# Router stage of a fused attention and expert kernel: rows split in place, 16-bit turning, residual kept unscaled

## The chip, the cores and the metric

One Trainium2 chip, one core of it. The metric is the device time of one execution in microseconds (us). Engines are named as in the profile: PE (TensorE, with PEld for its weight loads), DVE (VectorE), ACT (ScalarE), POOL (GpSimd) and SP (SyncE, which here only issues DMAs).

## What is computed

The kernel computes a whole two-layer model over 2048 tokens of 512 numbers. What matters here is the last block, the mixture of experts, and how it is fed:

```python
# x: the residual after layer 1's attention, [2048, 512]
x = _layernorm(x_in)                     # handed to the block
aff = sigmoid(x @ wa)                    # wa: [512, 16]
topk_p, topk_i = top_k(aff, 2); topk_p /= sum(topk_p)
routed = sum over the two chosen experts of topk_p * expert(x)
shared = sum over two shared experts of expert(x)
expert(x) = w2(gelu(x @ g + gb) * (x @ w1 + b1)) + b2
return x_in + (x + shared + routed)      # so the residual and the normed row are both added
```

With m the mean and r the inverse deviation of a row, the normed row is `r*x_in - m*r`, so what is added to the experts' results is `(1 + r)*x_in - m*r`. The kernel calls `1 + r` the gain and `-m*r` the shift.

## The kernel before, in words

The kernel is a row of stages, each a block in which every engine runs its own program and engines meet by semaphores; between two stages all engines meet. The tokens are 16 tiles of 128. In order: long convolution, a ternary feed-forward, keys and values, attention (`stage_attention`, L1575), the router (`stage_router`, L2044), a stage that chooses experts and runs the two shared ones (`stage_route_and_shared`, L2199), and the routed experts in 47 blocks of 128 rows (`stage_experts`, L2624). The residual x lies in SBUF (`x_res`, 16 tiles of 128x512 f32) until the router ends; then its space becomes that of the experts' weights.

Products of wide numbers are made of two 16-bit parts, a high one and a low one (value minus high), with three matmuls (`three_products`, L1138): high by high, high by low, low by high.

**Attention.** The order of work is a list of steps (batch, unit) that all engines walk. Per batch SP loads the keys (L1654) and stacks the next queries in twelve small DMAs (`qs`, L1662), which PE needs for the first scores of the next batch (L1859). DVE adds the projection to x (`added`, L1781) and takes statistics (`statistics`, L1785). In the last batch it makes the means, scales and the first two normed tiles (`front`, L1547 to L1572).

**Router.** For tile t of 16:
- DVE makes `xn` (128x512 f32, two buffers) from x, mean and inverse deviation (L1571), two tiles ahead.
- ACT copies it to 16 bits, `rows` high (L2182); DVE takes the rest, `rows` low (L2125). SP stores both to `token_rows` in HBM (256 KB a tile, L2091), from which the expert stage later gathers. There are four buffers of rows (`SETS = 4`); ACT waits for the store of tile t-4.
- PE turns `xn` with four f32 transposes (L2158) into PSUM `ps_rx`. ACT copies that once as f32 (`r_xT`, L2186) and once as 16-bit high (`s_xT`, L2189); DVE takes the low (L2127). SP stores both parts of the first 12 tiles (`turned_tiles`, L2094).
- PE multiplies `r_xT` with the router's weights `wa` in f32, 16 columns, four matmuls (L2164, "xcount" in the profile is eight a tile).
- ACT makes gain*x + shift (L2193): in place for ten tiles, which SP stores to `mid_rows` (L2097); six tiles (chunks 6, 7 and 0) go to places that outlive x: `e_rows`, `s_x`, `e_yo`.

Beside it SP loads `wa` (L2078), the rows of biases (L2081, L2083) and six shared weights of 512 KB (L2086), which POOL casts to the high part (L2110) and DVE takes the low part of (L2131). At the end ACT makes exp of the logits (L2195) and DVE the sigmoid (L2145, L2146) and the low part of the biases (L2149).

**Later.** The shared experts' sum is added to x tile by tile on DVE (`add_sums`, L2427; for the two late chunks `add_shared`, L2847), the routed results in `add_results` (L2854, L2856). The biases of the down products come in by a product of a row of shares per token (`cols`, turned by PE) with `down_bias`.

```python
        self.xn = [sb(f"r_xn{i}", [P, D], F32) for i in range(2)]
...
                act.activation(scaled_x, k.x[:, t, :], ACT.Identity, bias=shift[:, t:t + 1], scale=gain[:, t:t + 1]).then_inc(added, 1)
```

Of the kernel before, what the change touches and what calls it, by code (L numbers as in the profile page):

```python
# [15 lines left out]
P = 128  # L16
# [1524 lines left out]

FRONT = 4
# [4 lines left out]
class RouterScales:  # L1547


    def __init__(self, sb, semaphore):  # L1550
        self.mean, self.var, self.tmp, self.rstd, self.gain, self.shift = (
            sb(f"r_{n}", [P, NT], F32) for n in ("mean", "var", "tmp", "rstd", "gain", "shift"))
        self.xn = [sb(f"r_xn{i}", [P, D], F32) for i in range(2)]
        self.var_ready, self.rstd_ready, self.scaled, self.xn_ready = (
            semaphore(f"rs_{n}") for n in ("var", "rstd", "sca", "xn"))

# [13 lines left out]
    def normalise(self, dve, x, t):  # L1570
        dve.tensor_scalar(self.xn[t % 2][:, :], x[:, t, :], self.mean[:, t:t + 1], self.rstd[:, t:t + 1], ALU.subtract, ALU.mult)\  # L1571
           .then_inc(self.xn_ready, 1)  # L1572


def stage_attention(k, ks, last_keys, v_hi, v_lo, qw, ow, vectors, x_mean, x_rstd, stats, qs, kb, ahead, front):  # L1575
# [3 lines left out]
    with ExitStack() as ctx:  # L1579
# [127 lines left out]
        def _(act):  # L1707
# [14 lines left out]
            for b, u in STEPS:  # L1722
# [23 lines left out]
                if u == 1 and queried(b + 2):  # L1746
                    act.wait_ge(shift_ready, 1)
                    for t in range(TPB):
                        tile = (b + 2) * TPB + t
                        act.activation(xn[t][:, :], xtile(tile), ACT.Identity, bias=x_shift[:, tile:tile + 1],  # L1750
# [257 lines left out]
E_N = 16  # L2008
SH_N = 2
FE = 256  # L2010
# [10 lines left out]
SETS = 4  # L2021
# [19 lines left out]
TURNED_STORES = EARLY[0] * ST  # L2041


def stage_router(k, stats, xaff, sgu, sd, down_bias, kept, front, x_places):  # L2044
# [4 lines left out]
    with ExitStack() as ctx:  # L2049
        sb = lambda name, shape, dt: ctx.enter_context(nc.sbuf_tensor(name, shape, dt))  # L2050
        two = lambda name, shape, dt: [sb(f"{name}{i}", shape, dt) for i in range(2)]
        wa = sb("r_wa", [P, DC, E_N], F32)
        gain, shift, xn, scaled, xn_ready = front.gain, front.shift, front.xn, front.scaled, front.xn_ready
        xT = two("r_xT", [P, DC, P], F32)
        rows = [sb(f"r_rows{i}", [P, 2, D], BF16) for i in range(SETS)]
# [3 lines left out]
        psX = [ctx.enter_context(nc.psum_tensor(f"ps_rx{i}", [P, D], F32)) for i in range(SETS)]  # L2059
        psL = ctx.enter_context(nc.psum_tensor("ps_rl", [P, NT * E_N], F32))  # L2060
        raw = [sb(f"r_raw{i}", [P, 1024], F32) for i in range(6)]
        w_loaded, w_high = [k.semaphore(f"r_w{i}") for i in range(6)], k.semaphore("r_whi")
        rows_high, rows_low = k.semaphore("r_rh"), k.semaphore("r_rl")
# [3 lines left out]
        wa_loaded, dve_step, added, x_psum, xT_ready, x_high, x_low, logits, exped = (  # L2067
            sem(n) for n in ("wa", "dve", "add", "xp", "xT", "xh", "xl", "log", "ex"))
        bias_zeroed, bias_loaded, bias_high, x_stored = (sem(n) for n in ("bz", "bl", "bh", "xst"))
        rows_stored, turned_stored = ([sem(f"{n}{i}") for i in range(SETS)] for n in ("rs", "ts"))  # L2070
        block = ctx.enter_context(nc.Block())
        chunks = lambda a: a.rearrange("p (c t) -> p c t", c=DC)
# [4 lines left out]
        def _(sp):  # L2077
            sp.dma_start(wa[:, :, :], k.ins["L1_ffn_wa"].rearrange("(c p) e -> p c e", p=P)).then_inc(wa_loaded, 16)  # L2078
            sp.wait_ge(bias_zeroed, 1)
# [4 lines left out]
            for n in range(6):  # L2084
# [29 lines left out]
        def _(dve):  # L2114
# [37 lines left out]
        def _(pe):  # L2152
# [937 lines left out]
```

## Time and profile before

| | |
|---|---|
| median of 3 runs | 1137.9 us (1137.3 to 1138.25) |
| profiled execution | 1144.85 us, its span 1143.1 us |
| PE / PEld busy in the span | 1029.8 us (90%) / 771.7 us (68%) |
| DVE / ACT / POOL busy | 845.9 us (74%) / 684.2 us (60%) / 582.2 us (51%) |
| mean granted clock of TensorE | 0.944 of full |
| DMA | 194.60 MB, mean 170 GB/s |

Times in rows are from the start of the span. "Busy" is the time in which an engine has an instruction in hand; a row's duration includes the fill and the drain, so instructions that follow each other closely overlap a little, and the distance between two starts is what one costs its engine. "Granted clock" is the share of TensorE's full 2.4 GHz that it was given. A bracket behind a row is the idle time before it and who ended that.

### The profile page before, as it was taken

Reading aid. Unit: us, or ns where it says so; the run is one execution under the profiler, and the core shown is the slowest. Engines: PE = TensorE matmul, PEld = TensorE weight load, DVE = VectorE, ACT = ScalarE, POOL = GpSimd, SP = SyncE. Lnnn points to the kernel's source line nnn. Section 1 sums busy time; section 2 is a strip of 40 time slices with the busy share of each in tenths; the row PEclk is TensorE's granted clock in tenths of the full one; section 3 lists DMA queues with packets and bytes.
Section 4 is the critical chain, followed back from the end, with each engine's and each line's share of the span. In section 5 each row is a group of like instructions: output and inputs, shape, how many; then the busy total and the mean of one; then the engine's idle time right before and its main releaser. Section 6 shows DMA issues by size and latency. Waiting matters only on the chain. (4 is left out here: it accounts for less than half of the span.)

```text
span 1143.1 us, 24593 instructions
## 1 busy us (share of the span) xinstructions
PE 1029.8 (90%) x9092; PEld 771.7 (68%) x9175; DVE 845.9 (74%) x1480; ACT 684.2 (60%) x1203; POOL 582.2 (51%) x635
## 2 busy tenths in 40 slices
PE   4899998689998998878999988789996999999997
PEld 4677776634443776557877766687673888888874
DVE  5589999869998788757888866698746455556548
ACT  4565773779886656567888764574543345545431
POOL 5444445425544344458778885303873355555520
PEclk9999999789999999979999998659999899999999
DMA  8584431869886223232222210764986577678879
GB/s 318 176 256 122 160 116 38 158 174 237 221 226 177 87 72 104 68 89 56 65 71 63 57 30 1 257 226 181 203 249 224 165 239 242 236 246 281 303 264 352
DMA packets 133705, 194.60 MB, mean 170 GB/s; under 512 B 67990, under 2 KB 70204, under 8 KB 132792
## 3 DMA queue, kind: packets, MB, share of 16 engines
q1 hardware_dynamic: 117256, 149.45, 43.3%
q0 software_dynamic: 8544, 24.68, 7.0%
q10 hardware_dynamic: 7792, 18.96, 5.3%
q8 instruction: 71, 1.16, 0.4%
q14 instruction: 42, 0.34, 0.1%
HBM read 127.47 MB, written 44.48 MB: 150 GB/s over the span
## 5 line engine op out<-in xcount | busy, mean ns | idle before, releaser
L470 PE MATMUL ps_y<-kv,toep 128*128 128x288 f32 x640 | 156.5, 407 | 5.2 <-DMA toep<-taps_padded 3.2
L470 PEld LDWEIGHTS ps_y<-kv,toep 128*128 128x128 f32 x640 | 121.2, 190 | 40.0 <-DMA toep<-taps_padded 4.7
L164 POOL TENSOR_TENSOR kv<-kx 128x1024 f32<-128x1024 f32 x32 | 60.6, 1893 | 85.9 <-DVE outT L524 37.7
L1808 DVE TENSOR_REDUCE at_negmax<-ps_s 128x4 f32<-128x1024 f32 x64 | 78.1, 1220 | 32.0 <-PE ps_s L1859 32.0
L2684 POOL DMA_INDIRECT expert_results<-e_yo,target x47 | 69.7, 1482 | 58.1 <-ACT e_yo L2735 58.1
L1141 PEld LDWEIGHTS ps_eg<-e_xT,e_w 128*128 128x128 bf16 x1128 | 69.0, 100 | 15.1 <-DVE e_w L2789 2.5
L1141 PE MATMUL ps_eg<-e_xT,e_w 128*128 128x128 bf16 x1128 | 73.1, 223 | 4.0 <-DVE e_xT L2796 4.0
L1141 PE MATMUL ps_eu<-e_xT,e_w 128*128 128x128 bf16 x1128 | 72.2, 221 | 0.0
L2789 DVE COPY e_w<-expert_weights 128x4096 bf16 x47 | 57.7, 1227 | 19.3 <-issue 19.3
L2802 DVE SCALAR_TENSOR_TENSOR e_y<-ps_eu,e_bias,e_y 128x128 f32<-128x128 f32 x94 | 28.7, 346 | 55.1 <-PE ps_eu L1141 52.7
L2679 POOL DMA_INDIRECT e_rows<-token_rows,token x45 | 43.5, 967 | 49.9 <-PE ps_ex L2886 43.7
L1094 PE MATMUL ps_fH<-w1T,f_qaT 128*128 128x512 bf16 x256 | 64.2, 395 | 3.7 <-PEq L636 2.1
L1141 PEld LDWEIGHTS ps_eu<-e_xT,e_w 128*128 128x128 bf16 x1128 | 66.6, 99 | 0.0
L1110 PE MATMUL ps_fY<-w2T,f_qbT 128*128 128x512 bf16 x256 | 59.4, 387 | 4.0 <-DMA f_qbT<-f_qb 4.0
L2751 ACT ACTIVATE e_xT<-ps_ex 128x512 bf16<-128x512 bf16 x47 | 28.1, 597 | 57.5 <-PE ps_ex L2886 57.5
L1697 POOL TENSOR_TENSOR vw<-kw 128x1024 bf16<-128x1024 f32 x32 | 60.5, 1892 | 2.7 <-ACT kw L1738 2.7
L1697 POOL TENSOR_TENSOR vw<-at_pf 128x1024 bf16<-128x1024 f32 x32 | 60.6, 1893 | 0.0
L494 DVE TENSOR_TENSOR prod<-ps_y,qx 128x1024 f32<-128x1024 f32 x32 | 39.1, 1223 | 24.9 <-ACT ps_y L417 24.9
L1744 ACT ACTIVATE qs<-ps_m 32x256 bf16<-32x256 bf16 x128 | 48.0, 375 | 10.7 <-PE ps_m L1871 7.6
L2744 ACT ACTIVATE e_y<-ps_eg,e_bias 128x128 f32<-128x128 f32 x94 | 29.4, 363 | 39.7 <-PE ps_eg L1141 26.0
L1055 POOL CAST f_dparts<-f_draw 128x1024 bf16<-128x1024 f32 x16 | 17.5, 1094 | 64.5 <-DVE f_qb L938 64.5
L1094 PEld LDWEIGHTS ps_fH<-w1T,f_qaT 128*128 128x128 bf16 x256 | 25.4, 100 | 36.8 <-issue 5.1
(450 smaller groups left out, 3086.8 us busy)
## 6 DMA issues: line engine op xcount, KB each, us to landing
e_parts<-down_parts SPq DMA_DIRECT2D x47, 512.0 KB
w_raw<-in_L_ffn_w ACTq DMA_DIRECT2D x32, 512.0 KB, 4.3
toep<-taps_padded SPq DMA_DIRECT2D x32, 256.0 KB, 3.5
f_draw<-in_L_ffn_rw SPq DMA_DIRECT2D x16, 512.0 KB, 4.5
down_parts<-f_dparts SPq DMA_DIRECT2D x16, 512.0 KB, 2.9
expert_weights<-expert_results SPq DMA_DIRECT2D x16, 512.0 KB, 11.2
x_res<-in_x SPq DMA_DIRECT2D x4, 1024.0 KB
c_in<-in_ctx SPq DMA_DIRECT2D x4, 1024.0 KB, 14.3
```

Source lines behind the costliest of these rows:

```text
L164: pool.tensor_tensor(pairs[:, :, :, 0:HD0], x[:, :, 0:HD0].unsqueeze(2).broadcast_to([P, ROWS_N, WIDE, HD0]), sliding_rows(x, 0, 1, WIDE), ...
L470: last = pe.matmul(y[:, l * B:(l + 1) * B, :, WIDE - 1:], toep[h % 2][:, (DC - 1 - l + m) * P:(DC - l + m) * P], kv[h % 2][:, m * B:(m + 1 ...
L494: dve.tensor_tensor(slots[:, :, 0:WIDE, :], blocks(y)[:, :, :, WIDE - 1:PITCH - 1], sliding_rows(q, 0, 1, WIDE), ALU.mult) .then_inc(prod_ ...
L1094: pe.matmul(psH[:, f, :].rearrange("p (a t) -> p a t", t=P), qaT[p][:, c, :], k.w1T[:, f * DC:(f + 1) * DC, c, :], start=(c == 0), stop=False)
L1110: last = pe.matmul(psY[p][:, :].rearrange("p (a t) -> p a t", t=P), qbT[p][:, c, :], k.w2T[:, :, c, :], start=(c == 0), stop=(c == FC - 1))
L1141: instruction = pe.matmul(out, stationary[a], moving[b], start=first and n == 0, stop=last and n == 2)
L1697: pool.tensor_tensor(pl[u % 4][:, :, :, :], pf[u % 4], ph[u % 4], ALU.subtract)\
L1744: act.activation(qs[nb % 2][STACK:, h0 + j, c, :], psM[rows, :, :].rearrange("p q t -> p (q t)"), ACT.Copy)\
L1808: dve.tensor_reduce(negmax[u % 2][:, :].rearrange("p (j q) -> p j q", j=2), psS[:, :, :, :], AX.X, ALU.max, negate=True).then_inc(max_read, 1)
L2679: pool.indirect_dma_start(out=rows[j % 2], out_offset=None, in_=k.scratch["rows"], in_offset=bass.IndirectOffsetOnAxis(ap=token[:, j:j + 1 ...
L2684: pool.indirect_dma_start(out=k.scratch["results"], out_offset=bass.IndirectOffsetOnAxis(ap=target[:, j:j + 1], axis=0), in_=yo[j % 2], in ...
L2789: dve.tensor_copy(w1[j % 2][:, :, :, :].rearrange("p h c f -> p (h c f)"), W[:, bass.ds(e, 1), :, :, :].rearrange("p o h c f -> p (o h c f ...
```

## The change

- **Rows.** `xn` has four buffers, and its columns lie chunk by chunk (the numbers c, c+4, c+8, ... of a row together). Each f32 is split in place: its upper 16 bits are the high part as they stand, and DVE writes value minus high over the lower 16 bits. No instruction makes the high part; `rows` is gone, and SP stores `xn` itself.
- **Normalising.** From tile 2 on ACT makes `xn` (one activation with scale r and bias shift), three tiles ahead.
- **Turning.** PE turns both halves in 16 bits, eight transposes a tile, to two PSUM tiles of which there are three sets (`TURNS = 3`); ACT copies the high, DVE the low. `r_xT` is gone, and the logits are made of three 16-bit products from the turned parts.
- **x kept unscaled.** Attention stores each tile of x to `mid_rows` as soon as it is done; the router has no L2193 and no L2097. Six tiles are loaded back from HBM to their later places (after the row store of tile 4). The gain is applied where the shared sum is added (`scalar_tensor_tensor`), for the last chunk where the first routed result is added; the shift comes in by three 16-bit parts in three columns of `cols` and three rows of ones in `down_bias`, made on POOL.
- **Loads.** `wa` and two shared weights are loaded when attention begins, the other four in its last but one batch; `at_xn`, `at_qn`, `at_sq`, `at_qhi` and `at_qlo` lie in that space before. ACT casts two of the six weights, POOL four.
- The layout of `token_rows` changes with `xn`, so the expert stage's transposes (L2886) read every second 16-bit number where they read every fourth.

```diff
+        self.xn = [sb(f"r_xn{i}", [P, D], F32) for i in range(SETS)]
...
+    def turning_halves(self, t, c):
+        a = self.xn[t % SETS][:, :].bitcast(BF16).rearrange("p (c i s) -> p c i s", c=DC, s=2)
+        return a[:, c, :, 1], a[:, c, :, 0]
...
@@ stage_attention, SP
+            sp.dma_start(front.wa[:, :, :], k.ins["L1_ffn_wa"].rearrange("(p c) e -> p c e", p=P)).then_inc(front.wa_loaded, 16)
+            for n in range(4, 6):
+                front.load_shared_weight(sp, k, n)
             for b, u in STEPS:
...
+                        if (b, u) == following(project_step(c, t, 1)):
+                            sp.wait_ge(y_added, tile + 1)
+                            sp.dma_start(mid_dram[tile, :, :], xtile(tile)).then_inc(front.mid_stored, 16)
+                if (b, u) == (B - 1, 4):
...
+                        front.load_shared_weight(sp, k, n)
@@ stage_router, SP
             for t in range(NT):
                 q = t % SETS
                 sp.wait_ge(rows_low, t + 1)
-                sp.dma_start(rows_dram[t, :, :], rows[q][:, :, :].rearrange("p s d -> p (s d)")).then_inc(rows_stored[q], 16)
...
+                sp.dma_start(rows_dram[t, :, :], xn[q][:, :].bitcast(BF16)).then_inc(rows_stored[q], 16)
+                if 0 < t <= TURNED_STORES:
...
+                if t == SETS:
+                    sp.wait_ge(front.mid_stored, 16 * NT)
...
+                            sp.dma_start(x_places[i](s), mid_dram[chunk * ST + s, :, :]).then_inc(x_back, 16)
@@ stage_router, DVE
+            def row_lows(t):
+                high, low = front.halves(t)
+                dve.wait_ge(xn_ready, t + 1)
+                dve.tensor_tensor(low, xn[t % SETS][:, :], high, ALU.subtract).then_inc(rows_low, 1)
+
+            def turned_lows(t):
...
+                dve.tensor_copy(turned[q][:, 1, :, :], psX[t % TURNS][1][:, :, :]).then_inc(x_low, 1)
@@ stage_router, ACT
+            def normalise(t):
+                act.wait_ge(scaled, 2 if t < FRONT else 4 if t < LAST.start else 6)
+                if t >= SETS:
+                    act.wait_ge(rows_stored[t % SETS], 16 * (t // SETS))
+                    act.wait_ge(x_psum, t - SETS + 1)
+                act.activation(xn[t % SETS][:, :].rearrange("p (c i) -> p c i", c=DC), k.x[:, t, :].rearrange("p (i c) -> p c i", c=DC),
+                               ACT.Identity, bias=shift[:, t:t + 1], scale=front.rstd[:, t:t + 1]).then_inc(xn_ready, 1)
...
             for t in range(NT):
+                if t + 3 < NT:
+                    normalise(t + 3)
                 act.wait_ge(x_psum, t + 1)
+                act.activation(turned[q][:, 0, :, :], psX[t % TURNS][0][:, :, :], ACT.Copy).then_inc(x_high, 1)
@@ stage_route_and_shared, DVE
-                    dve.tensor_tensor(x_tile(i, s), x_tile(i, s), psD[s][:, :], ALU.add).then_inc(d_added, 1)
+                    dve.scalar_tensor_tensor(x_tile(i, s), x_tile(i, s), gain[:, t:t + 1], psD[s][:, :], ALU.mult, ALU.add).then_inc(d_added, 1)
...
+            link(dve.tensor_copy(cols[:, :, SHIFT_AT], shift_parts[:, :, :]), wait=False)
```

How it moves ACT's instructions in the middle of the router. Before, a tile is four of them:

```order
L2182 ACTIVATE r_rows<-r_xn 128x512
L2186 ACTIVATE r_xT<-ps_rx 128x512
L2189 ACTIVATE s_xT<-ps_rx 128x512
L2193 ACTIVATE x_res<-x_res,r_shift,r_gain 128x512
L2182 ACTIVATE r_rows<-r_xn 128x512
```

Now (L2237 normalises, L2252 copies the turned high part, L2256 casts a shared weight):

```order
L2237 ACTIVATE r_xn<-x_res,stats,r_rstd 128x512
L2252 ACTIVATE s_xT<-ps_rx 128x512
L2237 ACTIVATE r_xn<-x_res,stats,r_rstd 128x512
L2252 ACTIVATE s_xT<-ps_rx 128x512
L2256 ACTIVATE sgu<-r_raw 128x1024
```

Two instructions a tile are left of four, and the normalising, which was DVE's, stands three tiles ahead of the copy behind it. SP's queue in the router, tiles 2 to 4 before:

```order
L2091 DMA token_rows<-r_rows 128x1024
L2094 DMA turned_tiles<-s_xT 128x1024
L2097 DMA mid_rows<-x_res 128x512
L2091 DMA token_rows<-r_rows 128x1024
L2094 DMA turned_tiles<-s_xT 128x1024
L2097 DMA mid_rows<-x_res 128x512
```

Now around tile 4:

```order
L2122 DMA token_rows<-r_xn 128x1024
L2126 DMA turned_tiles<-s_xT 128x1024
L2122 DMA token_rows<-r_xn 128x1024
L2126 DMA turned_tiles<-s_xT 128x1024
L2132 DMA s_x<-mid_rows 128x512 x2
L2132 DMA e_yo<-mid_rows 128x512 x2
L2132 DMA e_rows<-mid_rows 128x512 x2
L2122 DMA token_rows<-r_xn 128x1024
L2126 DMA turned_tiles<-s_xT 128x1024
```

Two DMAs of 256 KB a tile are left of three, and six loads of 256 KB stand between the row stores of tiles 4 and 5. On DVE a tile was L2125, L2127 and L1571; now it is L2164 (the row's low part) and L2172 (a copy of the turned low part):

```order
L2164 TENSOR_TENSOR r_xn<-r_xn 128x512
L2172 COPY s_xT<-ps_rx 128x512
L2179 TENSOR_TENSOR sgu<-r_raw,sgu 128x1024
L2164 TENSOR_TENSOR r_xn<-r_xn 128x512
L2172 COPY s_xT<-ps_rx 128x512
```

The six L2179 (before L2131) come in tiles 6 to 14, where they came in tiles 5 to 15.

## Rows read from the trace of the kernel before

**Rows 1.** Busy by stretch: us; PE, PEld, DVE, ACT, POOL; clock, DMA share, GB/s
```profile
719.50:768.70 49.20, 40.38 (x192) 39.53 (x192) 38.58 (x66) 37.07 (x66) 7.58 (x8) 0.51 0.75 270
581.00:608.00 27.00, 26.48 (x366) 21.57 (x368) 21.69 (x41) 22.11 (x40) 21.69 (x29) 1.00 0.24 60
```
**Rows 2.** Timeline of PE in the router: start us, us, engine, line, operation
```profile
721.41 1.97 PE L2158 MATMUL ps_rx<-ident,r_xn 128*128 128x128 f32 x8 [3.64 <-DMA r_wa<-in_L_ffn_wa]
...
748.70 1.09 PE L2158 MATMUL ps_rx<-ident,r_xn 128*128 128x128 f32 x4
749.59 1.73 PE L2164 MATMUL ps_rl<-r_wa,r_xT 128*128 128x16 f32 x8
751.15 1.09 PE L2158 MATMUL ps_rx<-ident,r_xn 128*128 128x128 f32 x4
...
761.85 3.43 PE L2164 MATMUL ps_rl<-r_wa,r_xT 128*128 128x16 f32 x16
```
**Rows 3.** Timeline of ACT, tile 4 of the router and the start of tile 5
```profile
735.95 0.63 ACT L2182 ACTIVATE r_rows<-r_xn 128x512 bf16<-128x512 f32 x1 [4.62 <-DMA token_rows<-r_rows]
...
736.96 0.59 ACT L2189 ACTIVATE s_xT<-ps_rx 128x512 bf16<-128x512 f32 x1
737.44 0.81 ACT L2193 ACTIVATE x_res<-x_res,r_shift,r_gain 128x512 f32<-128x512 f32 x1
738.15 0.63 ACT L2182 ACTIVATE r_rows<-r_xn 128x512 bf16<-128x512 f32 x1
```
**Rows 4.** Prices on PE: 128 columns in 16 bits, and 33 columns at half clock
```profile
907.72 0.61 PE L2886 MATMUL ps_ex<-ident_b,e_rows 128*128 128x128 bf16 x8
519.66 0.22 PE L1884 MATMUL ps_o<-v_hi,vw 128*128 128x33 bf16 x2
519.71 0.22 PE L1884 MATMUL ps_o<-v_hi,kw 128*128 128x33 bf16 x2
519.00:520.00 1.00, 1.00 (x23) 0.89 (x20) 0.49 (x2) 0.98 (x2) 0.92 (x3) 0.54 0.66 164
```
**Rows 5.** Timeline of DVE in the router, and the 16-bit copy of the expert stage
```profile
750.87 0.68 DVE L2125 TENSOR_TENSOR r_rows<-r_xn,r_rows 128x512 bf16<-128x512 f32 x1
751.47 0.68 DVE L2127 TENSOR_TENSOR s_xT<-ps_rx,s_xT 128x512 bf16<-128x512 f32 x1
...
754.47 1.22 DVE L2131 TENSOR_TENSOR sgu<-r_raw,sgu 128x1024 bf16<-128x1024 f32 x1
L2796 DVE COPY e_xT<-ps_ex x47: 410/414/425, 885.7 to 1095.2; 128x512 bf16<-128x512 bf16 x47
```
**Rows 6.** DMA issues and landings: 738 to 740, 757 to 763, and the row stores
```profile
DMA packets 438, 0.81 MB, mean 403 GB/s; under 512 B 48, under 2 KB 48, under 8 KB 437
token_rows<-r_rows SPq DMA_DIRECT2D x3, 256.0 KB, 2.0
DMA to landing us min/median/max: 2.0/3.5/9.2
```
**Rows 7.** DVE while POOL works on SBUF, and the same operation alone
```profile
728.26 1.52 DVE L2125 TENSOR_TENSOR r_rows<-r_xn,r_rows 128x512 bf16<-128x512 f32 x1
727.02 2.22 POOL L2110 CAST sgu<-r_raw 128x1024 bf16<-128x1024 f32 x2
```
**Rows 8.** Attention: SP's stacking, DVE's addition to x, and PE's wait
```profile
637.08 4.94 SPq L1662 DMA_DIRECT2D qs<-at_qhi  x8
633.46 0.69 DVE L1781 TENSOR_TENSOR x_res<-x_res,ps_p 128x512 f32<-128x512 f32 x1
674.36 0.61 PE L1859 MATMUL ps_s<-at_kb,qs 96*128 96x256 bf16 x4 [2.38 <-DMA qs<-at_qlo]
```
**Rows 9.** DVE's last instructions, and the two-input form with a factor per row
```profile
1136.78 1.22 DVE L2854 TENSOR_TENSOR expert_weights<-expert_weights 128x1024 f32<-128x1024 f32 x1
1139.29 1.28 DVE L2847 TENSOR_TENSOR expert_weights<-expert_weights,ps_ed 128x512 f32<-128x512 f32 x2
603.08 1.66 DVE L1826 SCALAR_TENSOR_TENSOR at_qn<-at_qn,vectors,ps_p 128x256 f32<-128x256 f32 x4 [0.29 <-PE ps_p L1935]
```

More of the change, by code:

```diff
@@ L2020 @@
 RAW_N = OWN_RAW + LENT_RAW
-SETS = 4
 LO_AT = 32
@@ L2050, in stage_router @@
         sb = lambda name, shape, dt: ctx.enter_context(nc.sbuf_tensor(name, shape, dt))
[L2051 to L2055, printed above, removed]
+        wa = front.wa
+        shift, xn, scaled, xn_ready = front.shift, front.xn, front.scaled, front.xn_ready
+        wa_parts = sb("r_wap", [P, 2, DC, E_N], BF16)
         turned = [kept[q // ST][:, q % ST, :, :].rearrange("p s (c t) -> p s c t", c=DC) for q in range(SETS)]
@@ L2159, in turn @@
                 last.then_inc(x_psum, 1)
             def score(t):
-                pe.wait_ge(xT_ready, t + 1)
+                pe.wait_ge(x_high, t + 1)
+                pe.wait_ge(x_low, t + 1)
                 for c in range(DC):
-                    last = pe.matmul(psL[:, t * E_N:(t + 1) * E_N], xT[t % 2][:, c, :], wa[:, c, :], start=(c == 0), stop=(c == DC - 1))
+                    last = three_products(pe, psL[:, t * E_N:(t + 1) * E_N], [turned[t % SETS][:, s, c, :] for s in range(2)],
+                                          [wa_parts[:, s, c, :] for s in range(2)], c == 0, c == DC - 1)
@@ L2621, in _, with stage_experts @@
             down(CN - 1)
-def stage_experts(k, out, sgu, sd, down_bias, shares, late_xT, late_loaded, W, bias_rows, expert, token, target, weight, rows, yo, fetched, stored):
+def stage_experts(k, out, sgu, sd, down_bias, shares, late_xT, late_loaded, W, bias_rows, expert, token, target, weight, rows, yo, fetched, stored, gain):
     nc = k.nc
@@ L2853, in add_results @@
                 dve.wait_ge(got_loaded[ORDER[n]], 32)
-                dve.tensor_tensor(x[:, tiles, :], x[:, tiles, :], got[:, tiles, 0, :], ALU.add).then_inc(first_added, 1)
+                if ORDER[n] == LATE[1]:
+                    for t in range(tiles.start, tiles.stop):
+                        last = dve.scalar_tensor_tensor(x[:, t, :], x[:, t, :], gain[:, t:t + 1], got[:, t, 0, :], ALU.mult, ALU.add)
+                else:
+                    last = dve.tensor_tensor(x[:, tiles, :], x[:, tiles, :], got[:, tiles, 0, :], ALU.add)
+                last.then_inc(first_added, 1)
                 dve.wait_ge(first_added, n + 1)
```

193 lines of the change are left out of this document (113 added, 80 removed).

## The prediction

> **What bounds the kernel now.** I looked first at the busy times by stretch [rows 1]. The router takes 49.2 us of the 1143.1 us span. PE has 40.4 us of it in hand, DVE 38.6, ACT 37.1, and the DMA engines are 75% busy: four parties near their limit, where attention beside it is a matter of PE alone (26.5 of 27.0 us). The granted clock differs too: 1.00 in attention, 0.51, which is the 1.2 GHz level, in the router, although PE always has an instruction in hand.
>
> The timeline of PE [rows 2] tells which of the four ends last. In the steady part a tile is four f32 transposes (748.70 to 749.59, 0.89 us) and eight f32 records of 16 columns (to 751.15, 1.56 us), without a gap: 2.45 us a tile. Sixteen tiles are 39.2 us. The rest of the 49.2 is the start (first transpose at 721.41, 1.9 us into the stage, waiting for `wa`), ACT's wait of 4.62 us for the first row store, which was queued behind 3 MB of shared weights [rows 3], and the tail: PE ends at 765.28, the stage at 768.70, 3.4 us later, for exp, the reciprocal and the bias. So what PE costs per tile is worth 16 times its size, until the next party binds.
>
> **The change, party by party, in us per tile.** I count start-to-start distances.
> - PE: eight 16-bit transposes. Eight of that size cost 0.61 us with their drain at 908, 0.056 apart [rows 4]; at half clock I double that, 8 x 0.11 = 0.89. Then 12 matmuls of 16 columns. Nearest row: 33 columns with a fresh 128x128 weight load each, at a granted clock of 0.54, start 0.05 to 0.06 per two [rows 4], so 12 x 0.028 = 0.34. Together 1.23 against 2.45.
> - ACT: two instructions instead of four. Normalising has the form of L2193, 737.44 to 738.15 = 0.71, the 16-bit copy 736.96 to 737.44 = 0.48 [rows 3]. Sum 1.19 against 2.2. Two weight casts of 1 us come on top.
> - DVE: the row's low part 0.60 (750.87 to 751.47) and a copy of 0.41 that I count 0.33 apart [rows 5]: 0.93. Six weight lows, 1.13 apart, are 0.42 a tile more: 1.35.
> - DMA: two transfers of 0.262 MB at the 403 GB/s of the busy stretch [rows 6]: 1.30. The transfers of x to HBM and the shared weights are gone from here, into attention, whose DMA share is 0.24 [rows 1].
> - The buffers. This is a loop, not an engine, and it is the largest: ACT normalises tile t+3 only when the row store of t-1 has landed; behind it in ACT's order stands the high copy of tile t; SP issues the turned store of t after that, and the row store of t+2 after the turned one; its landing frees ACT for t+6. Three tiles thus cost 0.71 + 0.59 + 0.32 (issue) + the landing. A lone row store lands after 2.0 us [rows 6]; with 0.65 us of turned tile ahead of it 2.65, so 4.27/3 = 1.42 a tile. With the median landing of 3.5 us [rows 6] it is 5.12/3 = 1.70. The trace has no such loop, since PE was always later; I take **1.55**, between the two, because the DMA engines would be some 84% busy at that pace, a little more than now.
>
> **The sum for the stage.** Start: two small DVE steps, a row low of 0.69, eight transposes, 2.0. Sixteen tiles at 1.55, 24.8. The six loads of x, 1.57 MB at 403 GB/s, are 3.9 us of queue between the row stores of tiles 4 and 5; with four buffers little is hidden: 3.5 (between 1.0, if the slack of the queue takes them, and 5.0). Last product 0.6. Tail 3.4, unchanged. POOL's four casts now run while DVE is on its way: 1.0. Together **35.3 us instead of 49.2, 13.9 gained**.
>
> On that last term: DVE's row low took 1.52 us instead of 0.69 while POOL's casts ran [rows 7]. The Trainium skill, "SBUF — State Buffer", on the engine ports, says that a DVE operation with two SBUF inputs and a GpSimd operation that reads SBUF hold one port pair each for its whole length, the other fully blocked. By that rule each of the four casts would cost DVE what the row shows; the trace agrees for the one that it has, and this speaks against moving four casts into the busy part.
>
> **What it costs elsewhere.** Attention: SP gets 16 stores and six weight loads. What could hurt is the stacking of queries, since PE already waited for it 2.38 us once [rows 8]. But the first store of a batch waits for DVE's addition, over at 634.15, and the stacking starts at 637.08 [rows 8]: the store is out before it, and the second one comes after it. I cost it at nothing; the cover is those 2.9 us. After the router: 12 additions become the form with a factor. That form took 0.415 us for 256 columns (1.66/4), the plain one 0.64 for 512 [rows 9]; with another 256 columns at one per ns the new one is 0.69, 0.05 to 0.09 more. DVE isn't what ends that stage, so I count 0.4 of 1.1. One small copy more, 0.2. At the very end two of 0.69 replace one of 1.22: 0.2, since DVE is last there [rows 9]. The expert stage's transposes run at 0.056 us each though they skip three numbers of four [rows 4]; skipping one of two I cost at nothing. Sum +0.8.
>
> **Result**: -13.1 us. The profiled span of 1143.1 becomes 1130.0; that execution (1144.85 us) was 0.6% above the median, and I take the difference as it is: 1137.9 - 13.1 = **1124.8 us**. A difference of 0.2%, 2.3 us, is about what a measurement of this kernel can tell from none.
>
> **Rivals.**
> 1. *The queue alone binds, 0.17.* Landings stay near 2 us, so the loop is never felt; 1.30 a tile, 20.8, the loads half hidden (1.5), no blocked port: 2.0 + 20.8 + 1.5 + 0.6 + 3.4 = 28.3, and +0.3 later: 1117.3. For it: only two transfers a tile. Against: the loads of x, and ACT's strict order.
> 2. *The port is blocked in full, 0.13.* Four casts x 0.83 (1.52 - 0.69) = 3.3 instead of 1.0: 1127.1. For it: the row. Against: DVE has 0.2 us of slack a tile to catch up. This is the rule of the page above.
> 3. *Slow landings, 0.15.* 1.70 a tile, loads 5.0, port 2.3: 2.0 + 27.2 + 5.0 + 0.6 + 3.4 + 2.3 = 40.5, +1.4 later: 1130.6.
> 4. *ScalarE pays for the column order, 0.06; the one that ends slower.* It now reads x in steps of four numbers (16 bytes) and must do so for 14 tiles; no row of ACT shows such a reading. Then ACT binds at normalise + 0.48, and the loads hide. Break-even is 48.4 - 6.0 = 42.4 us for 16 tiles, 2.65 each, so a normalising of 2.17 instead of 0.71, three times. At four times, 2.84, the stage is 6.0 + 16 x 3.32 = 59.1: **+10.7, 1148.6**. Against: all of ACT's rows at 512 numbers cost 0.48 to 0.71 whatever the types.
> 5. *Attention stalls, 0.03.* If the stores delay the stacking after all, by an issue and a transfer (0.32 + 0.65) in six batches, +5.8: 1130.6. That each weight load takes PE's time at half clock (0.11 and more for each of 20) is excluded by the 0.028 of rows 4.
>
> **How the numbers follow.** The forecast has 0.46. Its own bounds are 1.42 and 1.70 a tile (-2.1, +2.4) and the loads (-2.5, +1.5). The range runs from rival 1 to rival 3 with what lies about them, 1118 to 1132 us; left out are rival 4 and the outer halves of 1 and 3. Faster by over 0.2%: all but rival 4, 0.94. Rival 4 is slower in two cases of three, 0.04, and near break-even in one, 0.02.
>
> **What would show it.** The router's stretch at 33 to 38 us; PE 1.2 us busy a tile with gaps that end with DVE or ACT; the clock still at 0.5; ACT waiting for `token_rows` in most tiles, longest after tile 4, with some 4 us; DVE's row low at 0.69, some at 1.5 next to POOL's casts; the normalising at 0.81. Attention's 27.0 us a batch unchanged. Wrong would be: a normalising above 1 us, no wait of ACT for stores, or batches of attention longer than 27.0 us.

## The result, and the profile after

The changed kernel takes 1129.34 us (median of 4 runs, 1127.89 to 1130.59), the kernel before 1137.76 us beside it (4 runs, 1137.3 to 1138.25): ratio 0.9925, 95% interval 0.9908 to 0.9943, so 8.4 us faster. On a second chip the ratio was 0.9955 (0.9935 to 0.9974). The forecast was 1124.8 us: right in sign and inside its range, and too generous by 4.5 us. The saving itself was forecast at 13.1 us; 8.4 and, on the second chip, 5.2 were measured.

| | profile before | profile after |
|---|---|---|
| execution, span | 1144.85, 1143.1 us | 1128.63, 1126.9 us |
| before the router | 719.5 | 718.9 |
| router | 49.3 | 42.5 |
| routed tokens and shared expert | 114.4 | 108.8 |
| experts to the end | 259.9 | 256.7 |

After the change PE is busy for 1014.4 us of the span, DVE for 834.2, ACT for 675.3, POOL for 584.0. The two profiled spans differ by 16.2 us, the medians by 8.4. Only the router's saving repeats (6.8 us here, 9.2 between the second profiles of the two kernels); the experiments show that.

Busy times by stretch after the change, the router and the same batch of attention as in [rows 1], with the same columns:

```profile
718.85:761.30 42.45, 22.42 (x320) 18.32 (x320) 27.92 (x53) 28.03 (x35) 7.75 (x12) 0.51 0.60 219
581.00:608.00 27.00, 26.64 (x370) 21.60 (x369) 21.70 (x41) 22.11 (x40) 21.69 (x29) 1.00 0.30 78
```

Attention has the 16 stores and the weight loads (78 GB/s instead of 60) and loses nothing: PE is as full as before, and four batches, from one load of keys to the fourth after it, take 108.4 us instead of 108.5 (542.60 to 650.97, before 542.44 to 650.91). In the router PE fell from 40.4 to 22.4 us, DVE from 38.6 to 27.9, ACT from 37.1 to 28.0, the DMA share from 0.75 to 0.60. **No engine is busy for more than two thirds of it**, so the 42.5 us must be read from a timeline. PE first, which answers to [rows 2]:

```profile
728.81 0.49 PE L1141 MATMUL ps_rl<-r_wap,s_xT 128*128 128x16 bf16 x12
729.15 1.01 PE L2211 MATMUL ps_rx<-ident_b,r_xn 128*128 128x128 bf16 x8
730.50 0.49 PE L1141 MATMUL ps_rl<-r_wap,s_xT 128*128 128x16 bf16 x12 [0.33 <-ACT s_xT L2252]
...
757.38 0.47 PE L1141 MATMUL ps_rl<-r_wap,s_xT 128*128 128x16 bf16 x12 [0.53 <-DVE s_xT L2172]
761.38 1.01 PE L1141 MATMUL ps_sg<-s_xT,sgu 128*128 128x256 bf16 x4 [3.53 <-PEq L2088]
```

Products 728.81 to 729.15: the 0.34 of the prediction. Eight turnings last 1.01 with their drain, and where products follow at once these start 0.81 to 0.83 later (0.89 in the prediction). But a tile starts every 1.69 us (728.81 to 730.50), and PE waits for ACT. ACT, which answers to [rows 3]:

```profile
721.51 0.57 ACT L2252 ACTIVATE s_xT<-ps_rx 128x512 bf16<-128x512 bf16 x1
725.28 1.31 ACT L2237 ACTIVATE r_xn<-x_res,stats,r_rstd 128x512 f32<-128x512 f32 x1 [3.20 <-issue]
726.49 0.58 ACT L2252 ACTIVATE s_xT<-ps_rx 128x512 bf16<-128x512 bf16 x1
726.97 1.30 ACT L2237 ACTIVATE r_xn<-x_res,stats,r_rstd 128x512 f32<-128x512 f32 x1
...
733.72 1.04 ACT L2256 ACTIVATE sgu<-r_raw 128x1024 bf16<-128x1024 f32 x1
741.17 1.29 ACT L2237 ACTIVATE r_xn<-x_res,stats,r_rstd 128x512 f32<-128x512 f32 x1 [6.41 <-issue]
...
756.26 0.60 ACT L2252 ACTIVATE s_xT<-ps_rx 128x512 bf16<-128x512 bf16 x1 [1.20 <-PE ps_rx L2211]
```

Two things are to be seen. The normalising takes 1.31 us and not 0.81; start to start it is 1.21, with the copy's 0.48 the 1.69 of the cadence, and ACT has no gap between: **ACT is the pace**. And there are two holes, 3.20 us ahead of tile 4 and 6.41 us ahead of tile 9 (its record says "issue", so the profile names nobody; in the program ACT waits there for a row store's landing, and in pe_stepped, one of the experiments below, the record of the first hole names it). SP's queue in that stretch tells what stands in front of those stores:

```profile
719.98 2.55 SPq L2116 DMA_DIRECT2D r_braw<-in_L_ffn_rb  x3
722.57 0.57 SPq L2118 DMA_DIRECT2D r_braw<-in_L_ffn_sb  x2
723.18 0.82 SPq L2122 DMA_DIRECT2D token_rows<-r_xn  x2
...
730.83 0.94 SPq L2132 DMA_DIRECT2D s_x<-mid_rows  x2
731.82 0.91 SPq L2132 DMA_DIRECT2D e_yo<-mid_rows  x2
732.76 0.91 SPq L2132 DMA_DIRECT2D e_rows<-mid_rows  x2
733.72 0.43 SPq L2122 DMA_DIRECT2D token_rows<-r_xn  x1
...
DMA to landing us min/median/max: 2.0/2.4/7.4
```

The rows of tile 0 were split by 719.7, but their store is issued at 723.18, behind five loads of bias rows that nobody needs before 758. The six loads of x stand behind the store of tile 4 as written; the row stores after them land after up to 7.4 us, where the median is 2.4 (last line, of the row stores).

The stage as it was: start and first hole, to 725.28, 6.4; twelve tiles at 1.69, 20.3; two weight casts 1.9; second hole 6.4; from ACT's 753.92 to PE's end at 757.85, 3.9; tail to 761.3, 3.4. Together 42.3 of 42.45.

### The profile page after: what moved, and what is told of

Its sections match the earlier page's. It is cut to its first block and busy times, and to the rows that moved or that the text cites. A ratio compares the mean times of both kernels' runs of the same rounds, so it can differ in the third digit from the quotient of the medians.

```text
span 1126.9 us, 24929 instructions
## 1 busy us (share of the span) xinstructions
PE 1014.4 (90%) x9303; PEld 748.4 (66%) x9303; DVE 834.2 (74%) x1469; ACT 675.3 (60%) x1172; POOL 584.0 (52%) x639
## 5 line engine op out<-in xcount | busy, mean ns | idle before, releaser
L164 POOL TENSOR_TENSOR kv<-kx 128x1024 f32<-128x1024 f32 x32 | 60.6, 1893 | 83.0 <-DVE outT L524 35.3
L1141 PE MATMUL ps_ed<-e_parts,e_yhi 128*128 128x512 bf16 x188 | 55.9, 379 | 0.4 <-DVE e_ylo L2876 0.4
```

Source lines behind the costliest of these rows:

```text
L164: pool.tensor_tensor(pairs[:, :, :, 0:HD0], x[:, :, 0:HD0].unsqueeze(2).broadcast_to([P, ROWS_N, WIDE, HD0]), sliding_rows(x, 0, 1, WIDE), ...
L1141: instruction = pe.matmul(out, stationary[a], moving[b], start=first and n == 0, stop=last and n == 2)
```

## The experiments

The theory at this point: ACT pays for steps in SBUF and sets the pace, and the holes come from the order of the queue, that is from bursts in front of the row stores. Rivals: the queue itself binds; the holes are chance; one side of the steps is free. The stages in all profiles, in us (router: from the first MEMSET of `r_braw` to the first IOTA of `s_iota_e`; experts: from the first IOTA of `e_places` to the end of the span):

| kernel | ahead | router | routed, shared | experts | span |
|---|---|---|---|---|---|
| before | 719.5 | 49.3 | 114.4 | 259.9 | 1143.1 |
| before_again | 720.1 | 48.9 | 109.4 | 258.7 | 1137.1 |
| after | 718.9 | 42.5 | 108.8 | 256.7 | 1126.9 |
| after_again | 720.2 | 39.7 | 111.6 | 258.3 | 1129.8 |
| write_stepped | 718.2 | 39.8 | 109.1 | 256.8 | 1123.9 |
| bias_late | 721.0 | 39.4 | 108.3 | 259.6 | 1128.3 |
| back_last | 719.3 | 37.5 | 108.3 | 259.5 | 1124.6 |
| back_bias | 719.6 | 37.9 | 109.1 | 258.9 | 1125.5 |
| spread | 718.6 | 36.7 | 108.1 | 256.5 | 1119.9 |
| spread_again | 714.7 | 36.2 | 112.8 | 259.4 | 1123.1 |
| spread_dve | 717.7 | 40.6 | 108.6 | 256.4 | 1123.3 |
| pe_stepped | 721.4 | 39.0 | 108.5 | 260.4 | 1129.3 |
| pe_back_bias | 720.9 | 34.8 | 110.5 | 261.8 | 1128.0 |
| pe_spread | 718.0 | 33.8 | 107.2 | 261.4 | 1120.4 |

Read down the columns: the stages around the router move by 3 to 7 us between executions of kernels that are the same there, as much as most experiments on it bring. So verdicts come from the router's column and from rows, the ratios stand beside them.

### The steps: who pays for them (write_stepped, pe_stepped)

> The changed kernel, but ScalarE's normalising walks x in its own order (read step 4 bytes) and writes xn with a step of 512 bytes. Same values at the same places. Theory A (the 1.31 us of the normalising, where 0.81 was expected, is the price of reading in steps of 16 bytes): the activation falls to 0.81 us, unless a stepped write costs as much. Theory B (it is slow because it writes a buffer near others that PE and the DMA engines read): stays at 1.31. With 0.81 a tile costs some 0.4 us less where ACT binds, so 4 to 5 us of the router's 42.4 go.

```diff
-act.activation(xn[t % SETS][:, :].rearrange("p (c i) -> p c i", c=DC), k.x[:, t, :].rearrange("p (i c) -> p c i", c=DC),
+act.activation(xn[t % SETS][:, :].rearrange("p (c i) -> p i c", c=DC), k.x[:, t, :].rearrange("p (i c) -> p i c", c=DC),
```

> The changed kernel with xn's columns left in x's own order everywhere: ScalarE and VectorE read and write without steps, and the transposes (router's and the expert stage's) read the halves in steps of 16 bytes instead of 4. Theory A: normalising 0.81 us, router 4 to 5 us shorter. What speaks against it: if PE pays for steps of 16 bytes, the expert stage's eight transposes, 0.056 us each, grow; at double the price that is 47 x 0.45 = 21 us lost. I expect no change of them, since steps of 8 bytes cost nothing before.

```diff
-act.activation(xn[t % SETS][:, :].rearrange("p (c i) -> p c i", c=DC), k.x[:, t, :].rearrange("p (i c) -> p c i", c=DC),
+act.activation(xn[t % SETS][:, :], k.x[:, t, :],
...
-        a = self.xn[t % SETS][:, :].bitcast(BF16).rearrange("p (c i s) -> p c i s", c=DC, s=2)
+        a = self.xn[t % SETS][:, :].bitcast(BF16).rearrange("p (i c s) -> p i c s", c=DC, s=2)
```

The same for the two tiles that DVE normalises, and for the turnings of the expert stage. The group of ACT's normalising (ns: min, median, max), first in the changed kernel, with DVE's two tiles and the weight loads of the expert stage's turnings:

```profile
L2237 ACT ACTIVATE r_xn<-x_res,stats,r_rstd x14: 1284/1313/1381, 718.9 to 752.2; 128x512 f32<-128x512 f32 x14
L1583 DVE TENSOR_SCALAR r_xn<-x_res,r_mean,r_rstd x2: 735/736/737, 713.2 to 713.8; 128x512 f32<-128x512 f32 x2
L2961 PEld LDWEIGHTS ps_ex<-ident_b,e_rows x376: 97/98/147, 870.2 to 1078.5; 128*128 128x128 bf16 x188
```

in write_stepped, which reads in order and writes in steps of 512 bytes:

```profile
L2237 ACT ACTIVATE r_xn<-x_res,stats,r_rstd x14: 1254/1275/1316, 718.3 to 748.8; 128x512 f32<-128x512 f32 x14
```

and in pe_stepped, both sides in order:

```profile
L2237 ACT ACTIVATE r_xn<-x_res,stats,r_rstd x14: 802/812/819, 721.4 to 750.7; 128x512 f32<-128x512 f32 x14
L1583 DVE TENSOR_SCALAR r_xn<-x_res,r_mean,r_rstd x2: 536/536/537, 716.1 to 716.6; 128x512 f32<-128x512 f32 x2
L2961 PEld LDWEIGHTS ps_ex<-ident_b,e_rows x376: 142/145/166, 868.9 to 1080.9; 128*128 128x128 bf16 x188
```

The steps cost ACT 0.50 us an instruction (1.31 against 0.81) on the reading side, and nearly as much on the writing side (1.275). DVE paid too: 0.736 in the changed kernel, 0.536 here. That the order of the columns is the cause is shown: pe_stepped's instruction reads and writes the same buffers beside the same neighbours, and nothing else of it differs. That leaves nothing for theory B.

PE reads 16-byte steps at a price as well, which I hadn't expected: its weight load of a turning takes 145 ns, against 98 with the changed kernel's steps of 4 bytes (x376 in both). Eight turnings are 0.66 us instead of 0.61, and from one block of the expert stage to the next it is 4.47 us instead of 4.42 (941.78 to 946.25, in the changed kernel 941.05 to 945.47), so 47 blocks lose some 2.3 us. The whole expert stage was 260.4, 261.8 and 261.4 us in the three kernels that turned so, 256.4 to 259.9 in the eleven others, 3.0 less on average. So pe_stepped won 0.5 us of pace per tile, hid part of it in its holes (one of 6.93 us after the six loads), and gave 2 to 3 us back later: 1129.16 us (ratio 0.9958, 0.9943 to 0.9973), no better than write_stepped's 1127.95 (0.9944, 0.9924 to 0.9964), beside 1134.33 of the kernel before. Its record of the hole ahead of tile 4 names what ACT waits for:

```profile
727.40 0.81 ACT L2237 ACTIVATE r_xn<-x_res,stats,r_rstd 128x512 f32<-128x512 f32 x1 [3.33 <-DMA token_rows<-r_xn]
```

### The holes, one at a time (back_last, bias_late)

> The changed kernel, but the six loads of x from HBM are issued behind the row store of tile 15 instead of tile 4. Theory A (they stand in the queue before the row store of tile 5, and ACT waits 6.4 us for it): that wait is gone or under 1 us, and tiles run at 1.7 us throughout; the stage's end now waits for the loads, issued at some 2 us before PE is done and landing 5 to 6 us later, so 1 to 3 us are given back: net 3 to 5 us shorter. Theory B (ACT's pace binds and the wait is only slack used up): no change.

```diff
-                if t == SETS:
+                if t == NT - 1:
                     sp.wait_ge(front.mid_stored, 16 * NT)
```

1127.9 us, ratio 0.9945 (0.9925 to 0.9966); router 37.5 against 42.5 and 39.7. The six loads now stand behind the last row store. ACT, from the store of tile 4 on, has no hole:

```profile
733.37 0.59 ACT L2252 ACTIVATE s_xT<-ps_rx 128x512 bf16<-128x512 bf16 x1
733.84 1.05 ACT L2256 ACTIVATE sgu<-r_raw 128x1024 bf16<-128x1024 f32 x1
734.79 1.29 ACT L2237 ACTIVATE r_xn<-x_res,stats,r_rstd 128x512 f32<-128x512 f32 x1
735.98 0.59 ACT L2252 ACTIVATE s_xT<-ps_rx 128x512 bf16<-128x512 bf16 x1
...
751.51 0.38 ACT L2258 ACTIVATE r_exp<-ps_rl 128x256 f32<-128x256 f32 x1 [1.03 <-PE ps_rl L1141]
751.79 0.62 ACT L2260 ACTIVATE down_bias<-r_braw 128x512 bf16<-128x512 f32 x1
756.74 1.28 ACT L2597 ACT_TABLE_LOAD   x1 [4.32 <-PEq L2088]
```

A part comes back as a new wait: from PE's end (751.47) to the end of the stage (756.7) it is 5.3 us instead of 3.4, since the stage now ends when the loads have landed.

> The changed kernel, but the five small loads of the bias rows are issued behind the row store of tile 8 instead of ahead of that of tile 0. Theory A (3.2 us of issuing hold back the first row store, issued 4.3 us after the stage's start, and ACT then waits 3.2 us for it): the wait falls to 1 us or less, 2 to 3 us shorter. Theory B (it only uses up slack that the later wait after tile 4 takes back): under 1 us.

```diff
-            sp.wait_ge(bias_set, 1)
-            for at in (0, LO_AT, HI_AT):
-                sp.dma_start(bias_raw[at:at + E_N, :], ...)
...
+                if t == 8:
+                    sp.wait_ge(bias_set, 1)
+                    for at in (0, LO_AT, HI_AT):
+                        sp.dma_start(bias_raw[at:at + E_N, :], ...)
```

1130.14 us, 0.9971 (0.9956 to 0.9987), router 39.4. Against the one profile of the changed kernel (42.5) that looked like 3.1 us; against its second one (39.7) it is nothing. The wait ahead of tile 4 is 1.52 us, not the 1 or less expected, against 3.20 and 1.92; the one ahead of tile 9, which this edit doesn't touch, is 4.23 against 6.41 and 4.18. So about half of the 3.1 us is in the other hole. This experiment alone decides nothing.

### Both kernels again, and both holes away (before_again, after_again, back_bias, pe_back_bias)

> The kernel before once more, for a second profile of it. The stage of the routed tokens and the shared expert (from the first IOTA of s_iota_e to the first of e_places) took 114.4 us in the one profile of the kernel before, and 108.8, 109.1, 108.5, 108.3 and 108.3 us in the profiles of the changed kernel and four forms of it. If that belongs to the change: again 113 to 115 us. If it was that one execution: 108 to 110 us. The router stage must come out at 49 us (within 1) either way.

The routed stage took 109.4 us. **The 5.6 us that it seemed to have gained belonged to that one execution, not to the change.** The router was 48.9.

> The changed kernel beside the others on one chip: ratio to before 0.990 to 0.994 as in its first comparison, router stage 42.5 us (within 1.5), the two holes of ScalarE (3.2 us ahead of tile 3 or so, 6.4 us after the six loads of x) again in it. If the holes were chance of one profile, the stage would be under 38 us.

1131.54 us (9 runs) beside 1136.77 (20 runs), ratio 0.9955: a smaller gain than the 0.990 to 0.994 expected, and the router is further from 42.5 than the 1.5 us I allowed. Both holes are there again, smaller: 1.92 and 4.18 us instead of 3.20 and 6.41. That is 3.5 us less of holes, and the router is 2.8 us shorter (39.7 and 42.5):

```profile
725.30 1.33 ACT L2237 ACTIVATE r_xn<-x_res,stats,r_rstd 128x512 f32<-128x512 f32 x1 [1.92 <-issue]
...
739.32 1.29 ACT L2237 ACTIVATE r_xn<-x_res,stats,r_rstd 128x512 f32<-128x512 f32 x1 [4.18 <-issue]
```

Over both profiles the router is 41.1 against 49.1 us: 8.0 saved, where the medians say 8.4 and 5.2. No other stage shows an effect outside its own spread.

> Both holes taken away: the six loads of x come after the row store of tile 15, the loads of the bias rows after that of tile 8; nothing else differs. If the holes add up and nothing new shows (my theory): 42.5 - 5.0 (what back_last gave) - 3.1 (what bias_late gave) = 34.4 us of router, 16 tiles at 1.69 and a tail of some 5 us that waits for the six loads; the time 5 to 8 us below the changed kernel's on the same chip. Rival, the queue binds once the holes are gone: 10 MB at 0.4 MB/us is 25 us, so that would show as a DMA share near 1.0 through the stage and a router over 36. Rival, other stages give it back (experts 259.5 against 256.7 us): the time within 2 us of the changed kernel's.

The diff is that of back_last and that of bias_late. 1127.61 us against 1131.54 of the changed kernel on the same chip (ratio to before 0.9924, 0.9904 to 0.9944): 3.9 us less, where I expected 5 to 8. Router 37.9, not 34.4: **the two gains do not add up.** The rival that the queue itself binds isn't what shows: the DMA share is 0.69 over the stage, not near 1.0. The first row stores go out at 720.62, 1.0 us after the stage's start instead of 4.3, and yet ACT still waits 2.21 us ahead of tile 4:

```profile
722.28 0.60 ACT L2253 ACTIVATE s_xT<-ps_rx 128x512 bf16<-128x512 bf16 x1
725.09 1.31 ACT L2238 ACTIVATE r_xn<-x_res,stats,r_rstd 128x512 f32<-128x512 f32 x1 [2.21 <-issue]
...
757.46 1.28 ACT L2598 ACT_TABLE_LOAD   x1 [4.89 <-PEq L2088]
```

Late landings are the reason: of the first three row stores 2.6, 4.4 and 4.4 us. The DMA engines moved 377 GB/s from 721.5 to 722.5 and 16 GB/s from 723.5 to 724.5:

```profile
721.50:722.50 1.00, 1.00 (x10) 0.77 (x8) 0.81 (x5) 1.00 (x2) 0.00 (x0) 0.50 1.09 377
722.50:723.50 1.00, 0.04 (x1) 0.00 (x0) 0.91 (x3) 0.37 (x1) 0.92 (x2) 0.50 0.31 115
723.50:724.50 1.00, 0.86 (x9) 0.90 (x10) 1.00 (x2) 0.00 (x0) 1.00 (x2) 0.50 0.07 16
```

So it is neither the order of the queue nor its rate that makes this wait, but a landing that comes late with nearly nothing in flight. What holds it isn't settled, and nothing here tries it. It isn't one run's chance either: in the six runs whose first stores go out 1.0 us after the stage's start (bias_late, back_bias, pe_back_bias, spread, spread_again and pe_spread) the longest of the first three or four landings is 3.4 to 4.4 us; in the changed kernel it is 2.7 and 4.2. The end waits for the six loads as in back_last (4.89 us on ACT, 2.55 in the changed kernel).

> As back_bias, and ScalarE reads and writes in order (xn keeps x's order), TensorE reads the 16-byte steps when it turns. ScalarE then needs 0.70 + 0.48 = 1.18 us a tile instead of 1.69, so something else binds. My theory: the queue, 512 KB a tile at 0.38 to 0.40 MB/us = 1.3 to 1.4 us a tile, router 29 to 32 us, against 34.4 with the steps in ScalarE. If TensorE's half clock and its weight loads of 166 ns bind: 8 x 0.166 + 0.49 = 1.8 us a tile, router 35 to 37 us. In the expert stage the 376 turnings take 6 ns longer each: 2.3 us at most given back if they lie on the path, none if hidden behind the gathers.

1125.9 us, ratio 0.9903 (0.9881 to 0.9925); router 34.8, 3.1 less than back_bias, experts 261.8. The rival in which TensorE's weight loads bind at 1.8 us a tile is refuted: eight such turnings take 1.06 us in the router (pe_spread), the changed kernel's 1.01 to 1.03. My number for the router (29 to 32) was too good: ACT has waits of 2.54 us ahead of tile 6 (for `token_rows`, as its record says) and 1.69 ahead of tile 11, and the end waits 5.6 us for the six loads. My 2.3 us for the experts is what the blocks give (0.05 us each, as in pe_stepped).

### The loads one by one (spread, spread_again, spread_dve, pe_spread)

> As back_bias, but the six loads of x go one by one behind the row stores of tiles 4, 6, 8, 10, 12 and 14, and the five of the bias rows behind those of tiles 5, 7, 9, 11 and 13. A tile then asks the queue for 512 KB, or 768 KB at every second: 640 KB on average, 1.6 us at 0.40 MB/us, under ScalarE's 1.69. My theory (ScalarE's 1.69 us a tile is the bound, and it was the burst that made the hole): no wait of ScalarE over 1 us after the first four tiles, the end of the stage no longer waits for the loads (5.6 us from the last product to the end in back_bias, 3.4 again here), router 35.5 us (34.5 to 36.5) against 37.9. Rival (the queue): 1.6 is so near to 1.69 that each load's extra 0.65 us shows; then waits of 0.3 to 0.6 us at every second tile, router 37 to 39 us.

```diff
+                if t in (5, 7, 9, 11, 13):
+                    at, rows = ((0, E_N), (LO_AT, E_N), (HI_AT, E_N), (E_N, SH_N), (LO_AT + E_N, SH_N))[(t - 5) // 2]
+                    sp.dma_start(bias_raw[at:at + rows, :], ...)
...
+                if t in (4, 6, 8, 10, 12, 14):
+                    i, h = divmod((t - 4) // 2, ST)
+                    sp.dma_start(x_places[i](h), mid_dram[KEPT_CHUNKS[i] * ST + h, :, :]).then_inc(x_back, 16)
```

1122.69 us (6 runs) where the kernel before took 1134.28 (21 runs): ratio 0.9914 (0.9884 to 0.9943). Router 36.7, against 37.9 of back_bias and 34.5 to 36.5 expected; I had expected no wait over 1 us behind the first four tiles, and there is one, ahead of tile 11:

```profile
735.92 0.59 ACT L2250 ACTIVATE s_xT<-ps_rx 128x512 bf16<-128x512 bf16 x1
738.50 1.29 ACT L2235 ACTIVATE r_xn<-x_res,stats,r_rstd 128x512 f32<-128x512 f32 x1 [1.98 <-issue]
...
755.25 1.28 ACT L2595 ACT_TABLE_LOAD   x1 [2.56 <-PEq L2088]
```

The end is back at 2.56 us of waiting: the loads have landed by then.

> The kernel spread once more, for a second ratio to the kernel before (first 0.9914, 0.9884 to 0.9943) and a second profile. If its gain over the changed kernel (0.9925 and 0.9955) is real: 0.988 to 0.993, router 36 to 37.5 us. If the wait of 1.98 us that was left near tile 9 is of the queue's making (a load of 256 KB, a bias row, the tile's own 512 KB and the row stores behind them), there is again one wait of 1 to 3 us between tiles 6 and 14; if it was chance, none.

1126.05 us beside 1136.18: ratio 0.9922 (0.9898 to 0.9945), router 36.2, and the wait ahead of tile 11 is there again with 1.65 us. So it isn't chance; that the queue's order there makes it is likely, but no run takes it away.

> As spread, but VectorE normalises the tiles in the loop (the same 16-byte read steps, tensor_scalar of 128x512), and ScalarE only copies: the change without its ScalarE part. VectorE has then 0.64 + 0.61 + 0.33 + 0.42 (its share of the weights' low halves) = 2.0 us a tile against 1.69 of ScalarE. Theory: cadence 2.0, router 35.5 + 16 x 0.3 = 40 us (39 to 42), the time 4 to 5 us over spread's. Rival (the queue binds, not ScalarE): the router within 1.5 us of spread's.

```diff
-                act.activation(xn[t % SETS][:, :].rearrange("p (c i) -> p c i", c=DC), k.x[:, t, :].rearrange("p (i c) -> p c i", c=DC),
...
+                front.normalise(dve, k.x, t)
```

1129.28 us, ratio 0.9964 (0.9942 to 0.9985), against 1122.69 of spread on the same chip: 6.6 us slower, of which the router's column shows 3.9. Router 40.6, in the 39 to 42 expected. In the loop DVE has one gap, of 0.71 us; else it is 2.72 us for a tile with a weight low and 1.59 for one without:

```profile
737.26 0.72 DVE L1583 TENSOR_SCALAR r_xn<-x_res,r_mean,r_rstd 128x512 f32<-128x512 f32 x1
737.90 0.72 DVE L2162 TENSOR_TENSOR r_xn<-r_xn 128x512 bf16<-128x512 f32 x1
738.52 0.41 DVE L2177 COPY s_xT<-ps_rx 128x512 bf16<-128x512 bf16 x1
738.85 0.73 DVE L1583 TENSOR_SCALAR r_xn<-x_res,r_mean,r_rstd 128x512 f32<-128x512 f32 x1
```

So once the holes are small, the busiest engine's work per tile sets the router, and the queue's 1.3 to 1.6 us does not. It also shows that ScalarE is the right place for the normalising even at 1.21 us.

> As spread, and the 16-byte steps are read by TensorE when it turns: ScalarE 1.18 us a tile. The queue then binds, at 1.6 us a tile where a load of x stands and 1.3 else. Router 31 to 34 us (pe_back_bias 34.8, with its end waiting 5.6 us for the six loads), expert stage 260 to 262 us as in the two kernels that turned so (260.4, 261.8), against 256.7 to 259.5 in the others: 2 to 3 us given back. So the time within 2 us of spread's.

1125.31 us, ratio 0.9922 (0.9899 to 0.9946). Router 33.8, the shortest of all; experts 261.4 against 256.5. Here ACT has six waits of 0.69 to 2.38 us in the loop, the two longest ahead of tiles 6 and 15, and between them a tile takes 1.24 us of PE (products 0.37, turnings 0.87; 727.50 to 728.74) next to ACT's 1.19: the landings are the next limit, and PE comes right behind. What the stage wins (2.9) the experts lose (4.9 in these two profiles, some 2.3 by the blocks). Between spread and pe_spread the medians don't decide (1122.69 and 1125.31, ranges 1121.7 to 1127.7 and 1122.05 to 1129.9).

The lowest ratios are those of pe_back_bias (0.9903, once) and spread (0.9914 and 0.9922); which of the two is better isn't decided. Both are faster than the kernel before. Against the changed kernel spread was never timed on one chip; its ratios lie below 0.9925 and 0.9955, their intervals overlap, and only the router's column (36.7 and 36.2 against 42.5 and 39.7) is clear.

## Why the prediction was right, and where it was not

**Right.** PE's step at the clock's lower level (0.51 again): 0.34 for the products, to the hundredth, and 0.81 to 0.83 for the turnings where I had 0.89. That PE would stop being the bound, though that it "always has an instruction in hand" was too strong (40.4 of 49.2 us). DVE's step: 0.62 to 0.65 and 0.33, where I had 0.60 and 0.33. The tail: 3.4 measured, 3.4 forecast. Attention at no cost: a batch takes 27.1 us as before, and the time ahead of the router didn't move outside its spread. The transfers: the queue alone (1.30 a tile) doesn't bind at 1.69.

**The range held, the picture did not.** Rival 3 (1130.6) comes nearest to the time. Its 5.0 for the loads was seen (5.3 in the mean), and its pace of 1.70 a tile was met, but by ACT's steps and not by slow landings: that part is luck. The signs that the prediction named speak against it: router 42.5 and 39.7 instead of 33 to 38, a normalising of 1.31 where above 1 was to be wrong, and ACT waiting long for row stores ahead of two tiles and not of most. The router saved 8.0 us in the mean of two profiles instead of 13.9.

**The step that failed is ACT's**, "normalising has the form of L2193, 0.71". It has not: L2193 reads and writes in order. The same instruction with 16-byte read steps is 1.21 start to start. I had this as rival 4, gave it 0.06 and priced it only at three and four times; it came at 1.7 times, so it set the pace (1.69 where I had 1.55) without coming near the break-even of 2.17. Twelve tiles in the middle at 1.69 instead of 1.55 are 1.7 us. The rival's mechanism was true, its size was wrong, and its "against" was empty: the rows that I cited for it had no steps either.

The Trainium skill, "Advanced Engine Details and Errata", "SBUF Cachelines", has the rule that the prediction left out: SBUF answers at full rate while successive accesses stay in one 16-byte line, and an access that goes to a new line each time pays. By it f32 numbers 16 bytes apart should be slow and 16-bit numbers 4 bytes apart free. The rows agree: 1.31 against 0.81 us on ACT, 0.736 against 0.536 on DVE, 145 against 98 ns on PE's weight loads. It gives no amount. The section also says that two accesses to a line are enough to hide the delay. Steps of 8 bytes make two to a line, and the kernel before shows 113 ns a weight load for them instead of 98: here the measurement decides. The blocks of the expert stage were no longer for it (4.42 us in both kernels).

**The loop of the four buffers** (1.42 to 1.70), which I took for the pace, is nowhere the pace in the steady part: with the median landing of 2.4 us it asks less than ACT does. What it does is turn each burst of the queue into a hole.

**The six loads of x**: 3.5 forecast (1.0 to 5.0), holes of 6.4 and 4.2 us seen. The term stood for the queue's 3.9 us less some slack; but SP issues five stores more behind the loads and their landings stretch to 7.4 us. With 6.4 the term lies outside its own bounds.

**The start**: I had 2.0 and the tile's own time; the hole of 3.2 (1.9) us ahead of tile 4 was in no term. The five loads of bias rows ahead of the first row store stand in the diff. back_bias shows that they are only a part of that wait: 2.2 us stayed without them. The kernel before had a wait for the first row store at the same place (4.62, [rows 3]), which I put down to the shared weights alone.

**The port**, 1.0: nothing on the path. POOL's four casts run from 722.45 to 727.01. DVE's row low took 1.23 and 0.99 us next to them and 0.71 to 0.76 else, so 0.8 us in all. Between the two DVE waited 2.15 us for ACT anyway, and behind the second ACT has no gap:

```profile
721.99 0.71 DVE L2164 TENSOR_TENSOR r_xn<-r_xn 128x512 bf16<-128x512 f32 x1
722.93 1.23 DVE L2164 TENSOR_TENSOR r_xn<-r_xn 128x512 bf16<-128x512 f32 x1
726.62 0.99 DVE L2164 TENSOR_TENSOR r_xn<-r_xn 128x512 bf16<-128x512 f32 x1 [2.15 <-ACT r_xn L2237]
```

The Trainium skill, "SBUF — State Buffer", on the engine ports, has the two engines block each other fully; the rows agree in kind, and no run here isolates by how much.

**Later stages**, +0.8: the form with a factor took 0.738 us where the plain one took 0.680, as forecast, and 12 of them and the rest are below what these runs can tell (the stages move by 3 us by themselves).

The sum against the stage: 35.3 forecast, 42.5 and 39.7 measured. Of the 5.8 us to their mean (41.1), the tiles with start and end, hole apart, are 1.9 (29.3, from 3.2 + 20.3 + 1.9 + 3.9, instead of 2.0 + 24.8 + 0.6): the steps, and ACT's two weight casts, which lie on the path now that ACT is the pace. The loads are 1.8 (5.3 in the mean less 3.5), the start's hole 2.6, small waits of the second profile 0.3, the port -1.0: 5.6 together, the rest is rounding. So the two holes, with 4.4, weigh more than ACT's step: the start's one stood in no term. That a hole comes from the queue's order is shown for the loads alone (back_last, spread).

## What to carry to other kernels

Price an instruction by a row with the same operation and the same steps in memory; where there is none, the change of steps is a term of its own, not a rival in the tail. In a loop with few buffers that are freed by stores, ask what stands ahead of each store in the queue: a burst of 1.5 MB cost 4 to 6 us at once, the same loads spread over the tiles some 2. And take a second profile of both kernels before a stage away from the change is explained: here 5.6 us vanished with it.

## What the runs showed of the hardware

- ScalarE, 128x512 f32 to f32: 0.81 us in order, 1.31 with 16-byte steps on the reading side, 1.275 with 512-byte steps on the writing side. DVE's tensor_scalar on 128x512 f32: 0.536 in order, 0.736 with 16-byte read steps.
- TensorE's weight load of a 16-bit 128x128 tile at the full clock: 98 ns with steps of 4 bytes, 113 with 8 bytes (the kernel before), 145 with 16 bytes. Eight turnings took 0.61 us at 4 and at 8 bytes, and 0.66 at 16.
- A row store of 256 KB landed after 2.0 us at the least, 2.4 in the median, and up to 7.4 behind six loads of the same size. Of the first three of the stage two took 4.4 us in back_bias, though the DMA engines moved only 16 GB/s in the last of these microseconds (723.5 to 724.5).
